# One core, a fused layer kernel: constants from two engines, other warm-up matmuls, an earlier load and a new list of steps

## The chip, the cores and the metric

The kernel runs on one core of a Trainium2 chip. The metric is the device time in microseconds, and the median of several runs is given. All data are float32. "us" is a microsecond.

## What is computed

Four sequences of 512 tokens with 256 features go through one layer. The tokens are taken in four chunks of 128, and each chunk depends on the one before it, since a small network of three weights per head is trained while the sequence is read. Cut to what matters:

```
xn   = layernorm(x)
qkv  = xn @ Wqkv                       # 4 heads of 64; also 2 heads of 128 for the window attention
q,k,v= silu(qkv); q,k = l2norm(q), l2norm(k)
lr   = softplus(xn @ Wlr + BASE_LR_INV); mom = sigmoid(xn @ Wm + bm)
for chunk in 4 chunks of 128 tokens:
    out  = (silu(q@W0.T) * (q@W2.T)) @ W1.T      # before the update
    dw0,dw1,dw2 = gradients(k, v, lr) + mean(mom) * M
    M = dw ; W = renorm(W + newton_schulz5(dw))  # five rounds of matmuls, 16 heads x 3 weights
ttt  = rms(out) * o_norm_g * silu(xn @ Ws + bs)
att  = windowed softmax attention (128 queries, 256 keys)
x    = x + layernorm((ttt + att) @ Wo)
x    = x + layernorm(gelu(layernorm(x) @ proj1.T + b1) @ proj2.T + b2)
```

## The kernel before, in words

Every engine runs the same hand-made list `ORDER` of about 690 steps in turn, and executes of each step only its own part: TensorE the matmuls, VectorE and ScalarE the evictions and elementwise work, GpSimd the powers (square roots are done there as `pow`) and some products. A step is named KIND.chunk.index. An engine that reaches a step whose inputs are not there waits, and all later steps of that engine wait behind it. `bank_plan` walks the same list and gives every matmul step one or two of the eight PSUM banks, those that are free the longest.

The steps of chunk 0 and the lines that matter here:

- LN1 (L1051 to L1062, GpSimd L1388 and L1393) takes the layer norm's statistics, LNX (L1068, L1075) normalizes, XT (L531, L538) transposes with `ident`, QK (L554) and VV (L563) are the projections. The VectorE part of VV (L1108, L1114) adds `small_bias` and so waits for seven small loads, counted in `ld_misc`.
- WI (L1334, L1338, ScalarE L1010) spreads the three weights, which six loads bring (`w_in`, shown as X), into W. SI (L861, L862) is the silu, NQ the sum of squares (ScalarE L874, VectorE L1120, GpSimd `pow` L1388), NR the reciprocal and the product (L1126, L1128, GpSimd L1388, shown as silu<-silu,rq). TR (L582) transposes, and VectorE copies six of the ten results (L1141).
- SP (L1046, written to `lr`) makes the learning rates. KL on GpSimd multiplies with them (shown as kl and vl). FW, DH, GB and OUT (L620, L608, L595, L634) are the forward pass and the gradients, EL and ELB (L1155, L1157, L1046, L1166) their elementwise part, DW (L653) the weight gradients, OE (L1180, L1191) and OY (L1199) the output, MU and MR (L1206, L1219) copy the gradients and take row sums, SS and SN (L1215, L1388 `fro`, L1224 to L1229) normalize them.
- TX, NA, NB, NX (L671, L680, L690, L702) are one Newton-Schulz round, five rounds for each of three weights. The VectorE part of NA is the write of A, which is the first reader of `eye`.
- F1 (L771) and F2 (L782) are the MLP, S and PT and PV (L721, L728, L737) the attention, WO, L2, NT (L752, L1319, L759) what lies between.

ScalarE has one function table loaded at a time. `table(name)` loads another where a step needs it: SILU for SI, GB, FW, EXP for SP and S, GELU for F1.

At the start GpSimd fills all constants (L1496 to L1514): the learning-rate bias, `ident`, `ones_blk`, `ones_avg`, `half`, `neg_half`, `mask`. The last fill raises `consts`, on which TensorE, ScalarE and VectorE wait before their first step. `wait_apart` also waits on `consts`. GpSimd then builds `eye` in four small sums before its first step. TensorE transposes `ident` 24 times (L797) before its first step. The sync queue issues, in this order, the rows and `wqkv`, small weights, seven small loads, the six weight loads (L468), `p1T`, `p2T`, `wo`, the rows again for the residual, and then the second chunk's rows (`rows_in(1)`, L483), once all of the first rows have been normalized.

Of the kernel before, what the change touches and what calls it, by code (L numbers as in the profile page):

```python
# [128 lines left out]
def steps(text):  # L129
# [12 lines left out]
    MR.0.0 MR.0.1 MR.0.2 OY.0 PT.0.1 QK.1.2 QK.1.3 SS.0.0 SS.0.1 PV.0.0 PV.0.1 S.0.2 S.0.3 VV.1.0 CT.0.0 CT.0.1 VV.1.1
    SS.0.2 SN.0.0 SN.0.1 SN.0.2 VV.1.2 PT.0.2 VV.1.3 WO.0.0 PT.0.3 TX.0.0.0 TX.0.0.1 TX.0.0.2 SI.1.0 SI.1.1 NA.0.0.0
    NA.0.0.1 NA.0.0.2 PV.0.2 PV.0.3 WON.0.0 WO.0.1 CT.0.2 NB.0.0.0 NB.0.0.1 NB.0.0.2 CT.0.3 WON.0.1 WO.0.2 WO.0.3
    NX.0.0.0 NX.0.0.1 NX.0.0.2 TX.0.1.0 TX.0.1.1 TX.0.1.2 WON.0.2 WON.0.3 L2.0.0 L2.0.1 L2.0.2 TR.1.0 TR.1.1 NA.0.1.0
    SI.1.2 NA.0.1.1 NA.0.1.2 NB.0.1.0 NB.0.1.1 NB.0.1.2 TR.1.2 TR.1.3 L2N.0.0 L2.0.3 L2N.0.1 L2N.0.2 NX.0.1.0 NX.0.1.1
    NX.0.1.2 NT.0.0 NT.0.1 NT.0.2 TX.0.2.0 TX.0.2.1 L2N.0.3 SM.1 TX.0.2.2 NT.0.3 LN1.2 NQ.1.0 SI.1.3 NA.0.2.0 NA.0.2.1
    NA.0.2.2 NQ.1.1 F1.0.0 F1.0.1 NB.0.2.0 NB.0.2.1 NB.0.2.2 LNX.2 NQ.1.2 NQ.1.3 F1.0.2 F1.0.3 NX.0.2.0 NX.0.2.1
    NR.1.0 NR.1.1 NX.0.2.2 NR.1.2 TX.0.3.0 F1.0.4 TX.0.3.1 TX.0.3.2 S.1.0 NA.0.3.0 NR.1.3 NA.0.3.1 KL.1.0 NA.0.3.2
    KL.1.1 F1.0.5 NB.0.3.0 NB.0.3.1 NB.0.3.2 NX.0.3.0 NX.0.3.1 NX.0.3.2 KL.1.2 TX.0.4.0 TX.0.4.1 TX.0.4.2 TR.1.4  # L150
    F1.0.6 MS.1 TR.1.5 TR.1.6 S.1.1 XT.2 TR.1.7 F1.0.7 NA.0.4.0 NA.0.4.1 NA.0.4.2 MM.1 NB.0.4.0 NB.0.4.1 SP.1 NB.0.4.2
# [82 lines left out]
def layer_kernel(nc, x, Wqkv, Wlr, Wm, bm, Ws, bs, Wo, w0, w1, w2, o_norm_g, qk_scale, qk_offset,  # L234
                 proj1T, proj1_bias, proj2T, proj2_bias, out):
    with ExitStack() as ctx:
# [15 lines left out]
        def sem(name):  # L252
            return ctx.enter_context(nc.semaphore(name))
# [1289 lines left out]
```

## Time and profile before

| | us |
|---|---|
| median of 3 runs | 389.87 |
| lowest, highest | 389.61, 390.98 |
| the profiled execution's own time | 389.76 |
| its span, first to last instruction | 388.0 |
| TensorE busy in it | 370.2 (95%) |
| VectorE busy | 268.7 (69%) |
| ScalarE busy | 223.0 (57%) |
| GpSimd busy | 189.7 (49%) |

A page of the profile lists the engines' busy time, the span in 40 slices, and the costliest groups of instructions. PE is TensorE's matmuls, PEld its weight loads, DVE is VectorE, ACT ScalarE, POOL GpSimd, SP the sync queue. A float32 matmul stands in the trace as two pieces, a transpose as one. A busy TensorE is not one at its peak, since the ends of matmuls are modelled: an overlapped piece counts as busy until its modelled end.

### The profile page before, as it was taken

To read this page: it belongs to the slowest core of one execution; us is meant where nothing else is said; L and a number is where in the kernel's file an instruction comes from. 1 tells how busy PE (TensorE), PEld (TensorE's weight loads), DVE (VectorE), ACT (ScalarE), POOL (GpSimd) and SP (SyncE) were. 2 spreads that over 40 slices of the span, in tenths; PEclk is the share of its full clock that TensorE was granted. 3 is DMA by queue.
4 is the path that set the end of the run, shared out by engine and by line. 5 is a ranking of instruction groups with operands and counts; after the bars stand their busy time and mean duration, and the time that the engine had idled before them with its cause. 6 is when DMAs were issued, how large, how long until landed. Compare 5 with 4: busy or idle time off the path is not lost.

```text
span 388.0 us, 15998 instructions
## 1 busy us (share of the span) xinstructions
PE 370.2 (95%) x6766; PEld 296.1 (76%) x6766; DVE 268.7 (69%) x720; ACT 223.0 (57%) x439; POOL 189.7 (49%) x274
## 2 busy tenths in 40 slices
PE   5877999999999999999999999999999999999994
PEld 5457768976878877889567898779887757988883
DVE  3479799875557679987737876986786783777024
ACT  2587666595873366658574356674369845624500
POOL 6189563646207663667635563452245440457114
PEclk9999999999999999999999999999999999999999
DMA  5862000000000000000040000000000020000101
GB/s 154 233 198 57 2 2 4 3 4 3 3 3 4 0 3 2 3 18 4 30 125 4 3 2 2 3 2 4 3 5 30 27 61 3 0 3 0 56 0 55
DMA packets 12342, 10.85 MB, mean 28 GB/s; under 512 B 4208, under 2 KB 11760, under 8 KB 12272
## 3 DMA queue, kind: packets, MB, share of 16 engines
q1 hardware_dynamic: 12272, 9.83, 8.4%
q8 instruction: 54, 0.88, 0.9%
q14 instruction: 16, 0.13, 0.1%
HBM read 7.73 MB, written 2.10 MB: 25 GB/s over the span
## 4 chain that ended last, share of the span: by engine, by line
PE 76%; DVE 11%; issue 4%; POOL 4%; SPq 3%; ACT 2%; DMA 1%; POOLq 0%; DVEq 0%; ACTq 0%
PE pair L771 14%; PE pair L782 13%; PE pair L702 6%; PE pair L690 6%; PE pair L680 6%; PE pair L671 5%; PE pair L752 4%; PE pair L582 3%; PE pair L563 2%; PE pair L737 2%; PE pair L721 2%; PE pair L554 2%; POOL fro L1388 2%; PE pair L620 1%; DVE h L1046 1%
## 5 line engine op out<-in xcount | busy, mean ns | idle before, releaser
L771 PE MATMUL pair<-xn2T,p1T 128*128 128x512 f32 (+1 forms) x160 | 59.0, 513 | 0.0
L782 PE MATMUL pair<-p2T,h 128*128 128x256 f32 x256 | 56.7, 379 | 0.0
L782 PEld LDWEIGHTS pair<-p2T,h 128*128 128x128 f32 x256 | 48.2, 190 | 6.4
L1393 POOL TENSOR_SCALAR var<-mv 128x1 f32<-128x1 f32 (+1 forms) x55 | 13.0, 236 | 70.0 <-DVE mv L1357 31.5
L1022 ACT ACTIVATE h<-pair,b 128x512 f32<-128x512 f32 (+1 forms) x40 | 24.0, 602 | 31.8 <-PE pair L771 31.7
L771 PEld LDWEIGHTS pair<-xn2T,p1T 128*128 128x128 f32 x160 | 28.9, 190 | 17.0 <-issue 14.8
L813 ACT ACT_TABLE_LOAD x29 | 37.2, 1283 | 2.2 <-PEq L1533 1.7
L1046 DVE SCALAR_TENSOR_TENSOR A<-pair,eye 128x512 f32<-128x512 f32 x45 | 28.3, 682 | 10.3 <-PE pair L680 10.0
L1388 POOL TENSOR_TENSOR rstd<-var,neg_half 128x1 f32<-128x1 f32 (+1 forms) x55 | 32.8, 596 | 4.6
L1046 DVE SCALAR_TENSOR_TENSOR B<-pair,eye 128x512 f32<-128x512 f32 x45 | 28.4, 683 | 7.2 <-PE pair L690 7.2
L1388 POOL TENSOR_TENSOR nq<-ssq,half 128x8 f32<-128x8 f32 (+1 forms) x16 | 23.6, 1485 | 15.6 <-DVE ssq L1120 15.6
L554 PE MATMUL pair<-wqkv,xnT 128*128 128x512 f32 x64 | 29.8, 600 | 0.4 <-ACT xnT L806 0.4
L690 PEld LDWEIGHTS pair<-A 64*64 64x64 f32 x1440 | 23.6, 134 | 6.9 <-issue 4.2
L947 ACT ACTIVATE X<-pair 128x512 f32<-128x512 f32 x36 | 19.7, 601 | 15.1 <-PE pair L702 15.0
L702 PEld LDWEIGHTS pair<-X,B 64*64 64x64 f32 x1440 | 23.4, 134 | 6.1 <-issue 4.6
L690 PE MATMUL pair<-A 64*64 64x64 f32 x1440 | 25.9, 221 | 0.7 <-issue 0.4
L806 ACT ACTIVATE XT<-pair 128x512 f32<-128x512 f32 x45 | 24.2, 609 | 4.2 <-PE pair L671 4.1
L680 PEld LDWEIGHTS pair<-XT 64*64 64x64 f32 x1440 | 22.6, 135 | 4.8 <-issue 4.4
L702 PE MATMUL pair<-X,B 64*64 64x64 f32 x1440 | 25.6, 221 | 0.2
L1388 POOL TENSOR_TENSOR kl<-silu,lr 128x256 f32<-128x256 f32 x24 | 14.4, 621 | 23.0 <-issue 23.0
L680 PE MATMUL pair<-XT 64*64 64x64 f32 x1440 | 24.7, 220 | 0.3 <-DVE rows_b L1046 0.2
L671 PE MATMUL pair<-ident,X 128*128 128x128 f32 x180 | 23.4, 276 | 0.0
(164 smaller groups left out, 783.1 us busy)
## 6 DMA issues: line engine op xcount, KB each, us to landing
x<-in_L_attn_x_dram SPq DMA_DIRECT2D x4, 512.0 KB, 4.7
out_dram<-rows_a SPq DMA_DIRECT2D x16, 128.0 KB, 1.7
x_in<-in_L_attn_x_dram SPq DMA_DIRECT2D x3, 512.0 KB, 4.9
p1T<-in_L_ffn_proj_dram SPq DMA_DIRECT2D x1, 1024.0 KB, 5.4
p2T<-in_L_ffn_proj_dram SPq DMA_DIRECT2D x1, 1024.0 KB, 7.8
wqkv<-in_L_attn_Wqkv_dram SPq DMA_DIRECT2D x1, 768.0 KB, 4.6
x_in<-in_L_attn_x_dram SPq DMA_DIRECT2D x4, 128.0 KB, 4.3
wo<-in_L_attn_Wo_dram SPq DMA_DIRECT2D x1, 256.0 KB, 8.0
```

The source lines that it names most:

```text
L554: mm_ = pe.matmul(ps, xnT[:, k, b * P:(b + 1) * P], wqkv[:, k, 0:512], start=(k == 0), stop=(k == KC - 1))
L671: mm_ = pe.transpose(ps[:, b * P:(b + 1) * P], X[:, g, 2 * b:2 * b + 2, :], ident[:, :])
L680: mm_ = pe.matmul(BANK[bank[0] + row][64 * col:64 * col + 64, n * HD:(n + 1) * HD], xt, xt, start=True, stop=True)
L690: mm_ = pe.matmul(BANK[bank[0] + row][64 * col:64 * col + 64, n * HD:(n + 1) * HD], a, a, start=True, stop=True)
L702: mm_ = pe.matmul(BANK[bank[0] + row][64 * col:64 * col + 64, n * HD:(n + 1) * HD], B[64 * row:64 * row + 64, g, 4 * (row ^ (slot & 1)) + ...
L771: mm_ = pe.matmul(ps[:, at], p1T[:, k, n * P:(n + 1) * P], xn2T[:, k, at], start=(k == 0), stop=(k == KC - 1))
L782: mm_ = pe.matmul(ps[:, 0:DIM], h[:, n, b * P:(b + 1) * P], p2T[:, n, :], start=(n == 0), stop=(n == HC - 1))
L806: return act.activation(dst, src, ACT.Copy)
L813: act.preload_act_table_set(name)
L1022: act.activation(h[:, n, at], BANK[bank[0]][:, at], ACT.Gelu, bias=b1[:, n:n + 1]).then_inc(S["h"].sem, 1)
L1046: return dve.scalar_tensor_tensor(out=out_, in0=in0, scalar=scalar, in1=in1, op0=op0, op1=op1)
L1388: return pool.tensor_tensor(out_, in0, in1, op)
```

## The change

Constants. `ones`, a new 128x128 tile, is filled by VectorE, which then raises `warm`. VectorE also fills `neg_half`, `half`, `small_bias`, `ones_avg` and the four quarters of `ones_blk`, and raises `prepared`. GpSimd fills `ident` alone, selects its diagonal and raises `consts`. It then makes `mask` and raises `masks`, and waits for `prepared` before its first step. ScalarE and VectorE no longer wait for `consts` at the start. The build of `eye` becomes a step of its own, EY.0, between OE.0 and SS.0.0 on GpSimd. Where the other constants are read first, a wait is added: SS.0.0 on TensorE (`prepared`), VV.0.0 on VectorE (`prepared`), S.0.0 on VectorE (`masks`).

Warm-up. TensorE waits for `warm` and does 8 matmuls of `ones` with itself, in place of 24 transposes of `ident`, and then waits for `consts`.

Loads. `rows_in(1)` is issued behind the six weight loads and ahead of `p1T`.

List. All 686 steps of before remain, in another order, with EY.0 added. Of the start: WI.0 goes from before LN1.0.3 to behind NQ.0.1 on VectorE, and from before SI.0.0 to behind QK.0.3 on ScalarE; LN1.0.3 comes before LNX.0.1; LN1.1 comes before NQ.0.2 on GpSimd; SP.0 goes from before S.0.0 to behind TR.0.9 on VectorE; OUT.0 comes before QK.1.0 to QK.1.2; OE.0 comes before ELB.0.0; OY.0 comes before MR.0.0; PV.0.2, PV.0.3 and MS.1 come before the first A, WO.0.0 behind it. With the rules of `table` the list of before needs 29 table loads and the new one 26.

```diff
@@ sync @@
             sp.wait_ge(ld_qkv, 16)
...
+            rows_in(1)
             sp.dma_start(p1T[:, :, :], proj1T.rearrange("(k p) n -> p k n", p=P)).then_inc(ld_p1, 16)
...
-            rows_in(1)
             sp.wait_ge(*S["x_again"](0, 16))
@@ tensor @@
+                if c == 0 and g == 0:
+                    pe.wait_ge(prepared, 1)
...
+            pe.wait_ge(warm, 1)
+            for n in range(8):
+                pe.matmul(BANK[7][:, (n % 4) * P:(n % 4 + 1) * P], ones[:, :], ones[:, :], start=True, stop=True)
             pe.wait_ge(consts, 1)
-            for n in range(24):
-                pe.transpose(BANK[7][:, (n % 4) * P:(n % 4 + 1) * P], ident[:, :], ident[:, :])
             run(ORDER)
@@ scalar @@
-            act.wait_ge(consts, 1)
             run(ORDER)
@@ vector @@
+                    if c == 0:
+                        dve.wait_ge(prepared, 1)
                     dve.wait_ge(ld_misc, MISC)
...
+                if c == 0 and b == 0:
+                    dve.wait_ge(masks, 1)
...
-            dve.wait_ge(consts, 1)
+            dve.memset(ones[:, :], 1.0).then_inc(warm, 1)
+            dve.memset(neg_half[:, :], -0.5)
+            dve.memset(half[:, :], 0.5)
+            dve.memset(small_bias[:, 0:12], BASE_LR_INV)
+            dve.memset(ones_avg[:, :], 0.5 / CHUNK)
+            for r in range(2):
+                for k in range(2):
+                    last = dve.memset(ones_blk[64 * r:64 * r + 64, 64 * k:64 * k + 64], float(r == k))
+            last.then_inc(prepared, 1)
             run(ORDER)
@@ gpsimd @@
+            def EY(c):
+
+                pool.wait_ge(consts, 1)
+                for b in range(BATCH):
+                    last = tt(eye[:, b, :], ident[:, 0:HD], ident[:, HD:P], ALU.add)
+                last.then_inc(eyes, 1)
...
+            pool.memset(ident[:, :], 0.0).then_inc(zeroed, 1)
             pool.wait_ge(zeroed, 1)
             pool.affine_select(out=ident[:, :], in_=ident[:, :], compare_op=ALU.not_equal, fill=1.0, base=0,
-                               pattern=[[-1, P]], channel_multiplier=1)
-
+                               pattern=[[-1, P]], channel_multiplier=1).then_inc(consts, 1)
+            pool.memset(mask[:, :], 0.0).then_inc(zeroed, 1)
+            pool.wait_ge(zeroed, 2)
...
+                               pattern=[[1, P]], channel_multiplier=-1).then_inc(masks, 1)
+            pool.wait_ge(prepared, 1)
             run(ORDER)
```

The start of the list, before and after:

```diff
-    LN1.0.0 LNX.0.0 LN1.0.1 XT.0.0 XT.0.1 LN1.0.2 LNX.0.1 QK.0.0 LNX.0.2 XT.0.2 WI.0 LN1.0.3 VV.0.0 LNX.0.3 SI.0.0
-    QK.0.1 VV.0.1 NQ.0.0 SI.0.1 VV.0.2 NQ.0.1 XT.0.3 QK.0.2 VV.0.3 NR.0.0 NR.0.1 SI.0.2 NQ.0.2 MS.0 SM.0 LN1.1 QK.0.3
+    XT.0.0 LN1.0.0 LNX.0.0 LN1.0.1 LN1.0.2 QK.0.0 LN1.0.3 LNX.0.1 XT.0.1 SI.0.0 LNX.0.2 LNX.0.3 VV.0.0 QK.0.1 XT.0.2
+    VV.0.1 NQ.0.0 XT.0.3 SI.0.1 VV.0.2 NQ.0.1 QK.0.2 SI.0.2 QK.0.3 WI.0 NR.0.0 NR.0.1 TR.0.0 LN1.1 VV.0.3 NQ.0.2
...
```

## Rows read from the trace of the kernel before

**Rows 1.** The page: busy us of each engine, share of the span, instructions.

```profile
PE 370.2 (95%) x6766; PEld 296.1 (76%) x6766; DVE 268.7 (69%) x720; ACT 223.0 (57%) x439; POOL 189.7 (49%) x274
```

**Rows 2.** Windows: start and end, length, busy us of each engine, granted clock, DMA.

```profile
0.00:60.00 60.00, 49.44 (x518) 37.12 (x519) 42.48 (x125) 36.73 (x81) 38.41 (x60) 1.00 0.36 104
60.00:290.00 230.00, 229.22 (x5079) 185.31 (x5078) 173.21 (x449) 139.87 (x267) 112.89 (x152) 1.00 0.03 10
290.00:303.00 13.00, 12.45 (x415) 9.96 (x414) 9.02 (x24) 11.84 (x25) 5.97 (x8) 1.00 0.10 34
```

**Rows 3.** Chain that ended last, first 60 us: start, length, what.

```profile
11.44 2.22 DMA X<-in_L_attn_w_dram
...
18.77 3.27 POOL nq L1388 x2
...
49.87 1.78 DVE M L1206 x3
```

**Rows 4.** Timeline 0 to 20: start, length, engine, line, idle before and its releaser.

```profile
1.66 1.28 ACT L813 ACT_TABLE_LOAD   x1 [1.66 <-PEq L1533]
...
3.73 0.43 DVE L1051 BATCH_NORM_STATS2 st<-x_in 128x6 f32<-128x256 f32 x1 [3.73 <-POOL ones_blk L1514]
...
7.58 0.47 SPq L463 DMA_DIRECT2D b<-in_L_ffn_proj_bias_dram  x1
...
8.39 0.60 PE L531 MATMUL pair<-ident,rows_b 128*128 128x128 f32 x4
...
13.69 0.63 DVE L1334 COPY W<-X 128x128 f32<-128x128 f32 x4 [4.43 <-DMA X<-in_L_attn_w_dram]
...
16.04 0.63 ACT L861 ACTIVATE silu<-raw 128x512 f32<-128x512 f32 x1
```

**Rows 5.** Windows over the warm-up's matmuls (L797) alone.

```profile
4.00:7.60 3.60, 3.60 (x18) 1.00 0.79 233
7.80:8.50 0.70, 0.70 (x7) 1.00 0.17 58
```

**Rows 6.** DMA issues with us to landing, the one issued at 7.58.

```profile
b<-in_L_ffn_proj_bias_dram SPq DMA_DIRECT2D x1, 4.0 KB, 3.6
```

**Rows 7.** Line L1388, 18 to 33 us: ns min/median/max, first and last start.

```profile
L1388 POOL TENSOR_TENSOR nq<-ssq,half x4: 1633/1646/1652, 18.8 to 28.0; 128x8 f32<-128x8 f32 x4
L1388 POOL TENSOR_TENSOR silu<-silu,rq x4: 1040/1042/1044, 22.0 to 31.0; 128x512 f32<-128x512 f32 x4
L1388 POOL TENSOR_TENSOR rstd<-var,neg_half x1: 1063/1063/1063, 26.9 to 26.9; 128x4 f32<-128x4 f32 x1
```

**Rows 8.** Timeline 20 to 60.

```profile
22.07 1.00 DVE L1126 TENSOR_SCALAR nqe<-nq 128x8 f32<-128x8 f32 x1 [0.16 <-POOL nq L1388]
...
33.51 3.68 DVE L1141 COPY tttT<-pair 128x512 f32<-128x512 f32 x6
...
34.28 1.19 POOL L1388 TENSOR_TENSOR kl<-silu,lr 128x256 f32<-128x256 f32 x2
...
41.01 0.69 DVE L1155 TENSOR_TENSOR h<-A,pair 128x512 f32<-128x512 f32 x1 [2.32 <-ACT h L904]
...
54.77 1.13 DVE L1046 SCALAR_TENSOR_TENSOR rows_b<-pair,rsums,y 128x128 f32<-128x128 f32 x4
54.78 3.23 POOL L1388 TENSOR_TENSOR fro<-ss,half 128x8 f32<-128x8 f32 x2 [2.66 <-DVE ss L1215]
```

**Rows 9.** Timeline 55 to 76.

```profile
62.15 1.65 PE L680 MATMUL pair<-XT 64*64 64x64 f32 x96
...
62.99 1.89 DVE L1046 SCALAR_TENSOR_TENSOR A<-pair,eye 128x512 f32<-128x512 f32 x3
```

**Rows 10.** Timeline 284 to 304.

```profile
295.32 0.42 DVE L1275 CUSTOM_DVE_ANT_0 masked<-pair,mask 128x256 f32<-128x256 f32 x1 [0.69 <-issue]
...
295.64 1.28 ACT L813 ACT_TABLE_LOAD   x1
```

**Rows 11.** Timeline 340 to 360.

```profile
354.02 0.41 PE L759 MATMUL pair<-ident,rows_b 128*128 128x128 f32 x2 [0.33 <-DVE rows_b L1326]
```

More of the change, by code:

```diff
@@ L142 @@
[L142 to L151, printed above, removed]
@@ new lines @@
+    WON.0.1 CT.0.3 SI.1.3 WO.0.2 NX.0.0.0 NX.0.0.1 WO.0.3 NX.0.0.2 SM.1 WON.0.2 WON.0.3 TX.0.1.0 TR.1.0 TX.0.1.1
+    TX.0.1.2 L2.0.0 L2.0.1 MM.1 NA.0.1.0 NA.0.1.1 NA.0.1.2 NB.0.1.0 NB.0.1.1 L2N.0.0 TR.1.1 TR.1.2 NB.0.1.2 TR.1.3
+    NX.0.1.0 NX.0.1.1 L2.0.2 L2.0.3 NX.0.1.2 NT.0.0 NT.0.1 NT.0.2 TX.0.2.0 TX.0.2.1 L2N.0.1 L2N.0.2 L2N.0.3 TX.0.2.2
+    NT.0.3 NA.0.2.0 NA.0.2.1 NA.0.2.2 F1.0.0 F1.0.1 NB.0.2.0 NB.0.2.1 NB.0.2.2 F1.0.2 NQ.1.0 NQ.1.1 F1.0.3 LN1.2
+    NX.0.2.0 NX.0.2.1 NX.0.2.2 TX.0.3.0 TX.0.3.1 F1.0.4 TX.0.3.2 NQ.1.2 F1.0.5 NA.0.3.0 NR.1.0 NA.0.3.1 NA.0.3.2
@@ new lines @@
+    L2N.1.2 TX.1.2.0 TX.1.2.1 TX.1.2.2 L2N.1.3 NT.1.1 NT.1.2 NT.1.3 NQ.2.1 NA.1.2.0 NA.1.2.1 NA.1.2.2 SI.2.2 SI.2.3
+    F1.1.0 F1.1.1 NQ.2.2 NQ.2.3 NB.1.2.0 NB.1.2.1 NB.1.2.2 MS.2 F2N.0.0 F2N.0.1 F1.1.2 F1.1.3 F2N.0.2 NX.1.2.0 F2N.0.3
+    NR.2.0 SM.2 NX.1.2.1 NX.1.2.2 TX.1.3.0 TX.1.3.1 TX.1.3.2 F1.1.4 NA.1.3.0 NA.1.3.1 NR.2.1 NR.2.2 NR.2.3 NA.1.3.2
+    F1.1.5 NB.1.3.0 NB.1.3.1 NB.1.3.2 MM.2 NX.1.3.0 NX.1.3.1 NX.1.3.2 LN1.3 TX.1.4.0 TX.1.4.1 TX.1.4.2 TR.2.4 TR.2.5
+    KL.2.0 KL.2.1 SP.2 NA.1.4.0 NA.1.4.1 NA.1.4.2 TR.2.6 F1.1.6 LNX.3 NB.1.4.0 NB.1.4.1 NB.1.4.2 TR.2.7 F1.1.7 MP.2
@@ L184 @@
+    WO.3.2 CT.3.3 WON.3.0 WON.3.1 L2.3.0 L2.3.1 L2N.3.0 L2N.3.1 F2.2.2 F2.2.3 NT.3.0 NT.3.1 WO.3.3 WON.3.2 WON.3.3
+    L2.3.2 L2.3.3 L2N.3.2 L2N.3.3 F1.3.0.0 F2N.2.0 F2N.2.1 F2N.2.2 F2N.2.3 F1.3.1.0 F1.3.2.0 F1.3.3.0 F1.3.4.0
+    F1.3.5.0 NT.3.2 F1.3.6.0 NT.3.3 F1.3.7.0 F1.3.0.1 F1.3.1.1 F1.3.2.1 F1.3.3.1 F1.3.4.1 F2.3.0 F1.3.5.1 F1.3.6.1
+    F1.3.7.1 F2N.3.0 F2.3.1 F2.3.2 F2N.3.1 F2N.3.2 F2.3.3 F2N.3.3
 """)
@@ L401, in layer_kernel @@
         consts = sem("consts")
+        prepared = sem("prepared")
+        masks = sem("masks")
+        warm = sem("warm")
         eyes = sem("eyes")
@@ L1509, in _ @@
             pool.affine_select(out=mask[:, 2 * P:3 * P], in_=mask[:, 2 * P:3 * P], compare_op=ALU.is_ge, fill=NEG, base=0,
-                               pattern=[[1, P]], channel_multiplier=-1)
-            pool.memset(ones_blk[0:64, 0:64], 1.0).then_inc(zeroed, 1)
-            pool.wait_ge(zeroed, 2)
-            pool.memset(ones_blk[64:128, 64:128], 1.0).then_inc(consts, 1)
-            pool.wait_ge(consts, 1)
-            for b in range(BATCH):
-                last = tt(eye[:, b, :], ident[:, 0:HD], ident[:, HD:P], ALU.add)
-            last.then_inc(eyes, 1)
+                               pattern=[[1, P]], channel_multiplier=-1).then_inc(masks, 1)
+            pool.wait_ge(prepared, 1)
             run(ORDER)
```

80 lines of the change are left out of this document (36 added, 44 removed).

## The prediction

> **What bounds the kernel now.** I read the page first: TensorE is busy 370.2 us, 95% of the span of 388.0, and idle 17.8 [rows 1]. The windows say where. In the first 60 us TensorE lacks 10.6, from 60 to 290 it lacks 0.8 of 230, in 290 to 303 it lacks 0.5 [rows 2], and so about 5.9 are left for the end. Busy is overstated where pieces wait for each other, but the places are clear: time can be won at the start, a little at 290 to 303, and at the end. Elsewhere only a list that makes TensorE wait more, or less, can move anything.
>
> The chain of waits tells who rules the start. It runs over the sync queue's issues to the six weight loads, the last issued at 11.44 and landing 2.22 later, from there through WI and the silu to GpSimd's `pow` at 18.77, and at 49.87 it is still on VectorE (copies of M) [rows 3]. The timeline shows why: VectorE stood still 4.43 us in front of WI.0, with LN1.0.3 and the VV copies behind it, and the first silu came at 16.04 [rows 4].
>
> **The change part by part.** The sum is against the profiled execution's 389.76, which is 0.11 below the median of 389.87. I add 0.11 at the end.
>
> *Constants.* VectorE's first step began at 3.73, released by GpSimd's last fill [rows 4]. Now nine fills of its own stand in front of it. The trace shows no fill on VectorE. Its queue has more to do first than ScalarE's, which was free at 1.66 [rows 4], so I put it at 2.1 to 2.7, and I bound the fills by nothing and by half the 0.43 of its first statistics each: 2.1 to 4.6, likely 3.7, so no gain and at worst 0.9 lost there. Both ends stay hidden, as the next paragraphs show. The three added waits are for things ready by then, with tens of microseconds of cover at S.0.0 and SS.0.0. At VV.0.0 all later steps of VectorE, and ScalarE's first silu, are queued behind the wait, but the wait on the small loads next to it ends later.
>
> *Warm-up.* 24 pieces held TensorE until the first real transpose at 8.39 [rows 4]. They went 18 in 3.6 us, 0.20 each, and then 7 in 0.7, 0.10 each, while the clock column says 1.00 for both [rows 5]. By the pace that is the 1.2 GHz level up to about 7.7 us and the 2.4 GHz level after about 4 us of work. The new warm-up is 8 float32 matmuls, 16 pieces, at 0.20 about 3.3 us, from about 2.9 to 6.2. The first transpose comes 2 us earlier. Some early matmuls may run at half pace.
>
> *Where that gain stops.* The first silu needs VV.0.0's copy, and that needs the seventh small load, issued at 7.58 and landed 3.6 later [rows 4, 6]: 11.2. The projections are ready before that: QK.0.0 from 7.3, four pieces of 512 columns at 0.10 per 128 columns [rows 5], 1.7, then XT.0.1, then VV.0.0 with four of 276 columns, 0.9, so 10.4 with the gaps. So the silu starts at about 11.4 and not at 16.04, 4.6 earlier. It is WI.0's move that gives this, not the warm-up. On ScalarE two copies now come before the squares, so the first `pow` starts at 14.9, not 18.77: 3.9 earlier.
>
> *GpSimd to the last product.* Four `pow` at 1.65, four products at 1.04, and LN1.1's root, 1.06 and with the sum ahead of it about 1.3, are 12.1 [rows 7]. WI.0 (0.63 [rows 4] and two larger copies, about 1.4) now lies before NR.0.0 on VectorE, and LN1.1 stands before the third `pow`, which has to wait for it: together about 2.5 of gaps where before there were 1.2. The last product ends at 29.5, before at 32.0. Gain left: 2.5. The second chunk's rows, issued at about 12.1 behind the weights, are there in time, and `p1T` has 60 us of cover.
>
> *To the gradients.* The six copies that started at 33.51 start at 31.2, and the first EL at 38.7 and not 41.01 [rows 8]: 2.3 left. SP.0 is now behind these copies. KL, which waits for it, starts at 35.1, not 34.28 [rows 8], 0.8 later. KL is four times 1.19 and about 0.6, 7.1, and GpSimd's part of EL about 2.5: 44.7. That is still ahead of VectorE, whose copies of M began at 49.87 [rows 3] and now begin at about 48.
>
> *VectorE to the first A.* From 41.01 to 62.99 [rows 8, 9] VectorE is full (42.5 busy of 60, with most of the idle time before 16 [rows 2]). A gain in latency is here worth what VectorE has less to do. The new list puts PV.0.2 and PV.0.3 (two sequences, 1.13 [rows 8]) and MS.1 (about 0.4) ahead of the first A and takes WO.0.0 (0.6) away, 0.9 more. With MR waiting for OY the first A comes at 62.5. TensorE starts the round at 61.1 and not 62.15 [rows 9] and, since 0.9 of VectorE's work is already done, stays ahead. I book 1.3, with ends 0 and 2.4. EY.0, four sums, sits on GpSimd between OE.0 and SS.0.0, where GpSimd was idle 2.66 us before `fro` [rows 8]; it costs nothing, or its own 1.2 if that cover goes.
>
> *Chunk 2.* In before, S.3.0 stood in the fourth round: VectorE waited 0.69 for its scores with A queued behind, and ScalarE loaded a table at 295.64 inside the same round, while it was busy 11.84 of 13 [rows 2, 10]. The new list has S.3.0 in the fifth round, behind the last copies that the round needs from ScalarE. I book 0.6, with ends -1.5 (the loads now hold F1's banks) and 1.5.
>
> By the Trainium skill's page "ScalarE: Activation LUTs", section "What ACT_TABLE_LOAD costs", a switch takes a drain beside the load, about 2.66 us in all. The trace shows 1.28 [rows 10]. Three loads fewer are 3.8 us of ScalarE by the row and 8.0 by the page; at the page's price the sum would be about 1 us lower.
>
> *Chunk 3.* TensorE waited 0.33 for L2N.3.2 at 354.02 [rows 11]. The new list sends NT.3.2 behind six F1 halves. I book 0.1, with ends 0 and 0.4. The last steps behind F2.3.3 are unchanged.
>
> *The rest of the list* moves a few hundred steps by one to ten places over 230 us in which TensorE is full. I book 0, with ends -1.5 and 1.5.
>
> Sum: 389.76 - 1.3 - 0.6 - 0.1 = 387.76, plus 0.11 gives 387.9.
>
> **The rivals.**
>
> *A, the start's gain is absorbed.* VectorE is full from the first EL to the first A, and the order there costs what the latency saves. For it: my first A is only 0.5 earlier. Against it: TensorE needs less from VectorE after that. Booked 0.3 in place of all: 389.6, from 388.9 to 390.9.
>
> *B, the gain survives in full.* The 2.4 us at EL reach the first round, since VectorE's work between can be packed closer, and chunk 2 gives 1.5: 389.87 - 2.4 - 1.5 = 386.0, from 385 to 387.
>
> *C, slower: the clock.* The new warm-up ends at 6.2, and TensorE then has small gaps while rows come in. Between 6.4 and 18.3 it has 11 us of matmuls at full pace, nearly no slack. Each microsecond that it stays at the pace of the first row [rows 5] costs half a microsecond. The first 1 us of delay has cover; from about 12 on the start's gain of 1.3 is used up. At full pace only from 18.3 (12 us at half pace, 6 lost, 1 covered, with 1.3 and 0.7 won) the time is 389.9 + 5 - 2.0 = 392.9. For it: 24 pieces in a row came before the rise, now 16 with a gap after. Against it: the work goes on with gaps under 1 us.
>
> *D, shared reads.* A small VectorE instruction took 1.00 us at 22.07 for eight columns, about as long as the GpSimd product of 1.04 that ran beside it [rows 7, 8]. EY.0 and the later KL now run beside VectorE's fullest stretch. If these eight products and sums hold it 1.2 us, the start keeps 0.1: 389.1. The Trainium skill's page "GPSIMD Engine Reference", in its table of the engine, names the SBUF interfaces as shared with VectorE for instructions with two SBUF inputs; the row agrees that something is shared.
>
> **How the numbers follow.** Forecast, 0.38: 387.9, its own range 387.2 to 388.9. A 0.22 at 389.6. B 0.25 at 386.0. C 0.11 at 392.9. D 0.04 at 389.1. Half a per cent, about what a measurement tells from no change, is 1.95 us: faster means below 387.9. Half of the forecast's case and B are faster, 0.44. The other half, A and D are the same, 0.45. C is slower, 0.11. The range leaves out C and the lowest third of B, under 0.2: 385.3 to 390.9.
>
> **What would show it.** The first silu at 11 to 12 us; the last product at 29 to 30; the six copies of 33.51 at 31; the first A within 0.7 us of 62.99, lower; WI.0 without the 4.43 idle; 26 table loads; a round in chunk 2 without the 0.69; TensorE's pieces at 0.10 per transpose before 10 us. A first A later than 63, or QK.0.2 taking 3.6 us and not 1.9, would make the forecast wrong on the slow side. A first A at 61 would make it B.

## The result, and the profile after

The changed kernel took 387.73 us in the median of five executions (387.30 to 388.49), beside 389.87 for the kernel before (389.43 to 390.98). The ratio is 0.9943, with a 95% interval of 0.9929 to 0.9958. The profiled execution is the 388.49 one, with a span of 386.7. It is the slowest of the five. Twelve more executions of the same kernel, taken later and told below as e5, gave a median of 389.1 (387.01 to 391.41) beside 389.44, a ratio of 0.9984 (0.9962 to 1.0006), which does not exclude that nothing was won. There the new kernel's executions lie 4.4 us apart and the old one's 2.4 (389.00 to 391.36, 23 executions); this document explains only a part of that.

The page of the new kernel: busy us of each engine, and the table loads.

```profile
PE 369.2 (95%) x6758; PEld 294.9 (76%) x6758; DVE 271.5 (70%) x729; ACT 219.2 (57%) x436; POOL 191.7 (50%) x267
...
L820 ACT ACT_TABLE_LOAD x26 | 33.4, 1283 | 2.1 <-PEq L1548 1.7
```

Windows of the new kernel, with the columns of [rows 2].

```profile
0.00:60.00 60.00, 51.04 (x555) 38.62 (x559) 45.61 (x147) 40.04 (x87) 38.38 (x53) 1.00 0.35 104
60.00:290.00 230.00, 227.01 (x5073) 182.55 (x5064) 174.35 (x438) 130.76 (x255) 117.70 (x157) 1.00 0.05 15
290.00:303.00 13.00, 13.00 (x398) 10.91 (x397) 7.33 (x20) 11.50 (x24) 4.72 (x6) 1.00 0.02 4
```

Beside [rows 2], TensorE is 1.6 us busier in the first 60 us and busy through all of 290 to 303, but from 60 to 290 it now lacks 3.0 of 230, where before it lacked 0.8. The timeline of the first 61 us shows the new start: start, length, engine, line, what, and in brackets the idle time before and who ended it.

```profile
2.76 0.17 DVE L1389 MEMSET ones<- 128x128 f32 x1 [2.76 <-issue]
3.06 3.75 PE L803 MATMUL pair<-ones 128*128 128x128 f32 x16 [3.06 <-DVE ones L1389]
6.61 0.55 PE L535 MATMUL pair<-ident,rows_b 128*128 128x128 f32 x2
7.73 1.96 PE L558 MATMUL pair<-wqkv,xnT 128*128 128x512 f32 x4 [0.57 <-ACT xnT L813]
11.57 0.63 ACT L868 ACTIVATE silu<-raw 128x512 f32<-128x512 f32 x1 [0.98 <-DVE small L1122]
15.06 3.44 POOL L1406 TENSOR_TENSOR nq<-ssq,half 128x8 f32<-128x8 f32 x2 [5.41 <-DVE ssq L1128]
16.66 0.63 DVE L1344 COPY W<-X 128x128 f32<-128x128 f32 x4
...
27.78 1.04 POOL L1406 TENSOR_TENSOR silu<-silu,rq 128x512 f32<-128x512 f32 x1 [0.34 <-DVE rq L1136]
30.19 3.68 DVE L1149 COPY tttT<-pair 128x512 f32<-128x512 f32 x6
34.12 1.20 POOL L1406 TENSOR_TENSOR kl<-silu,lr 128x256 f32<-128x256 f32 x2 [3.07 <-issue]
37.68 0.69 DVE L1163 TENSOR_TENSOR h<-A,pair 128x512 f32<-128x512 f32 x1 [2.50 <-ACT h L911]
46.47 1.89 DVE L1214 COPY M<-pair 128x512 f32<-128x512 f32 x3
47.42 1.15 POOL L1406 TENSOR_TENSOR eye<-ident 128x64 f32<-128x64 f32 x4
...
59.63 1.67 PE L686 MATMUL pair<-XT 64*64 64x64 f32 x96
60.77 1.88 DVE L1052 SCALAR_TENSOR_TENSOR A<-pair,eye 128x512 f32<-128x512 f32 x3
```

WI.0's copies (16.66) no longer have 4.43 us of idle time in front of them, the first silu comes at 11.57 and not at 16.04 [rows 4], and TensorE's first round starts at 59.63, not at 62.15 [rows 9].

A ledger is the main tool from here on. It takes the start of the first NA piece of chunks 0, 1 and 2, the last F2 piece of chunk 2 and the last of chunk 3, from each kernel's timeline, and gives the first of these times and the four stretches between them. Chunk 3's column ends with its last F2 piece; about 6 us follow in every kernel. A profile is one execution; the median of all executions stands beside it, and beside that the median of before, measured together with it.

```
                 to NA.0.0  chunk 0  chunk 1  chunk 2  chunk 3   sum    median  before
before              62.15   100.32   100.06    90.34    29.15  382.02   389.87
after               59.63   101.60   101.72    88.34    29.46  380.75   387.73  389.87
e1  new code only   62.25   101.28    99.93    91.70    29.14  384.30   392.32  389.57
e2                  62.16   100.84    99.82    91.71    29.15  383.68   391.08  389.57
e3                  61.55   101.16   104.69    90.35    29.15  386.90   391.03  389.57
e4                  59.45   101.61   102.25    90.35    29.15  382.81   391.16  389.57
e5  after again     59.70   101.11   101.01    88.64    29.46  379.92   389.10  389.44
e6  S.3.0 back      63.08   101.07   100.90    92.99    29.46  387.50   394.89  389.44
e7  new from c2     62.64   100.32   100.29    88.50    29.46  381.21   388.92  389.44
e8  old start       63.13   102.22   101.09    88.75    29.45  384.64   392.30  389.44
e9  new list only   63.89   101.65   103.05    88.64    29.45  386.68   392.96  389.67
e10 MM.2 behind     59.70   101.13   101.05    88.13    29.46  379.47   388.39  389.67
e11 start and c2    60.48   101.31   100.04    88.16    29.46  379.45   387.08  389.67
e12 16 warm-ups     62.02   100.30    99.55    90.94    29.14  381.95   391.14  390.13
```

After against before: 2.5 won up to the first round, 1.3 lost in chunk 0, 1.7 lost in chunk 1, 2.0 won in chunk 2, 0.3 lost in chunk 3. Together 1.3 are won. The same kernel's other execution, e5, lost 0.8 and 0.95 in chunks 0 and 1 and won 2.1 in all, so one trace is good to about 1 us there.

The stretches do not hold the same work, since a new order moves steps across their ends. TensorE in chunk 2's stretch, of before and of after (start and end, length, busy us and pieces, clock, DMA): first everything, then the WO pieces (L752, L758), then the PV pieces (L737, L743).

```profile
262.53:352.87 90.34, 89.79 (x1892) 1.00 0.05 15
262.95:351.29 88.34, 88.34 (x1892) 1.00 0.05 15
...
262.53:352.87 90.34, 7.77 (x32) 1.00 0.05 15
262.95:351.29 88.34, 5.68 (x24) 1.00 0.05 15
...
262.53:352.87 90.34, 5.29 (x40) 1.00 0.05 15
262.95:351.29 88.34, 6.17 (x48) 1.00 0.05 15
```

Two WO steps have left the stretch and one PV step has come in, 1.2 us of work less. So of the 2.0 some 0.8 are a gain of chunk 2 itself; TensorE's idle time there went from 0.55 to nothing. One of the two WO steps lies now in chunk 3's stretch (four pieces, 1.03 busy), which is why that one is 0.3 longer although its idle time, 0.33 before, is gone too.

### The profile page after: what moved, and what is told of

Read it like the earlier page. It is cut to its first block, busy times and chain, and to the rows that moved or that the text cites. A ratio compares the mean times of both kernels' runs of the same rounds, so it can differ in the third digit from the quotient of the medians.

```text
span 386.7 us, 15982 instructions
## 1 busy us (share of the span) xinstructions
PE 369.2 (95%) x6758; PEld 294.9 (76%) x6758; DVE 271.5 (70%) x729; ACT 219.2 (57%) x436; POOL 191.7 (50%) x267
## 4 chain that ended last, share of the span: by engine, by line
PE 83%; DVE 8%; issue 3%; POOL 3%; ACT 2%; POOLq 0%; DVEq 0%; ACTq 0%
PE pair L788 14%; PE pair L777 14%; PE pair L708 6%; PE pair L686 6%; PE pair L696 5%; PE pair L677 5%; PE pair L558 5%; PE pair L743 3%; PE pair L586 3%; PE pair L758 3%; PE pair L567 3%; PE pair L727 3%; PE pair L734 2%; PE pair L657 2%; PE pair L624 1%
## 5 line engine op out<-in xcount | busy, mean ns | idle before, releaser
L1411 POOL TENSOR_SCALAR var<-mv 128x1 f32<-128x1 f32 (+1 forms) x55 | 14.1, 256 | 67.4 <-DVE mv L1367 30.5
L1406 POOL TENSOR_TENSOR fro<-ss,half 128x8 f32<-128x8 f32 x9 | 15.9, 1781 | 13.4 <-DVE ss L1223 13.4
```

The lines of the kernel that those rows point to most:

```text
L1406: return pool.tensor_tensor(out_, in0, in1, op)
```

## Experiments

The first four take the change apart. In all kernels with the new code and an old piece of list, EY.0 stands ahead of SS.0.0.

**e1: the new code, the old list.**

```diff
 # after's code
-ORDER = steps("""... the new list ...""")
+ORDER = steps("""... the old list, EY.0 ahead of SS.0.0 ...""")
```

> All of the change but the list: constants from two engines, 8 matmuls on ones, the earlier load of the second chunk's rows, with the list of before (EY.0 put ahead of SS.0.0). Theory, the move of WI.0 makes the start faster: here WI.0 still waits for the weights ahead of the first silu, so the silu stays at 16.0 us and the time at 389.8, within 0.4 of before. Rival, the shorter warm-up and the free GpSimd make the start faster: the first silu comes before 15 us and the time is 388.8 or less.

Measured: 392.32 (391.32 to 394.79), ratio 1.0074 (1.0046 to 1.0102). The start is as before. The loss sits in a few holes within groups of TensorE's pieces. Timeline of e1, TensorE alone:

```profile
73.67 1.50 PE L686 MATMUL pair<-XT 64*64 64x64 f32 x84
75.73 0.39 PE L686 MATMUL pair<-XT 64*64 64x64 f32 x10 [0.57 <-issue]
...
296.35 1.61 PE L686 MATMUL pair<-XT 64*64 64x64 f32 x92
299.33 0.33 PE L686 MATMUL pair<-XT 64*64 64x64 f32 x4 [1.36 <-issue]
```

84 pieces of one group of 96, then nothing for 0.57 us, then the rest: no wait of the program lies between them. "issue" says that nothing in the profile released the engine. With the old list the new code makes no part of the gain, and its loss is of a kind that the prediction did not have.

**e2: the same, with WI.0 behind NQ.0.1.**

```diff
 # e1's list
-... WI.0 LN1.0.3 VV.0.0 ... NQ.0.1 XT.0.3 ...
+... LN1.0.3 VV.0.0 ... NQ.0.1 WI.0 XT.0.3 ...
```

> As e1_code_only, with WI.0 alone moved behind NQ.0.1 in the list. Theory, WI.0's move is what wins the start: the first silu is at 11.4 to 12.5 us, GpSimd's last product before 30, the first round of Newton-Schulz starts 1.5 to 2.5 us before 62.15, and the time is 387.8 to 388.4. Rival, VectorE is full from the first EL on, and the gain is lost there unless the order of OE, OY and PV changes too: first round within 0.8 of 62.15, time 389.2 or more.

Measured: 391.08 (390.33 to 393.77), ratio 1.0039 (1.0021 to 1.0057). The first silu came at 12.39, but the first round at 62.16. The first silu is what the theory had, the first round (within 0.8 of 62.15) and the median (389.2 or more) are what the rival had. In this execution TensorE ran from 20 to 24 us at a granted clock of 0.59, so the trace may understate what moving WI.0 alone gives. The median is 1.2 below e1's, and the intervals of the two ratios overlap.

**e3: the new list up to NA.0.0.0, the old one behind. e4: the new list up to TX.2.0.0.**

```diff
 # e3: after's code
-ORDER = the new list
+ORDER = the new list up to NA.0.0.0, then the other steps in the old order
 # e4: after's code
-ORDER = the new list
+ORDER = the new list up to TX.2.0.0, then the other steps in the old order
```

> The changed kernel, with its new list up to the first NA.0.0.0 and all steps behind it in the order of before. Theory, the start's 2.5 us at the first round are kept where the rest of the list stays: first round at 59.6, time 387.4. Rival, TensorE's stream absorbs a part whatever the rest: time 388.5 or more.

> The changed kernel with its new list up to the first TX.2.0.0 and the order of before behind it, so chunk 2's rounds and chunk 3 are as before. Theory, the new order in chunk 2's rounds won 2 us (its profile is 0.4 behind at the third chunk's first round and 1.6 ahead at its end): time 389.5, 1.8 above the changed kernel. Rival, the 0.4 behind comes from one stall of 2 us at 203 us that this execution happened to have, and chunk 2 is worth 0.6 as booked: time 388.3.

Measured: e3 391.03 (389.29 to 394.65), ratio 1.0037 (1.0012 to 1.0061); e4 391.16 (390.20 to 394.51), ratio 1.0057 (1.0032 to 1.0082). The profiled execution of e3 was its slowest, with the clock at 0.50 from 28 to 32 us and a hole of 2.17 us at 180, so its medians count. The new start is worth 1.3 against e1, and there too the intervals overlap. In e3 WO.0.0 stands ahead of the first NA step, where after has it behind: of the 1.9 by which the first round is later than in after, 0.9 are this step. In e4 everything is as in after up to chunk 2, which then takes 90.35 and not 88.34, as in before. From e4 to after the sum falls by 2.1: that is what the new order behind TX.2.0.0 is worth, over chunks 2 and 3 and the end of chunk 1 together. e3's median falls to its rival (388.5 or more), and e4's lies above both its cases (389.5 and 388.3).

**e5: after once more, unchanged. e6: S.3.0 back in the fourth round.**

```diff
 # e6: after's list
-... TX.2.3.2 TR.3.3 SI.3.1 ... TX.2.4.2 NR.3.0 NR.3.1 NR.3.2 S.3.0 NR.3.3 ...
+... TX.2.3.2 TR.3.3 S.3.0 SI.3.1 ... TX.2.4.2 NR.3.0 NR.3.1 NR.3.2 NR.3.3 ...
```

> The kernel after once more, unchanged, beside the three below on one chip. In its first trace TensorE stood 2.0 us in front of NX.1.3.0 at 205.72, released by nothing that the profile shows (issue). Theory 1: this stall belongs to the program (its code and its place in the instruction stream); then it is there again within 0.3 us of its length and the median is again 387.3 to 388.2. Rival: it is an accident of one execution; then it is gone, the profiled span is 384.5 to 385.5, and the median, which is over many executions, stays at 387.3 to 388.2.

> The kernel after with one step moved: S.3.0 goes from the fifth round of chunk 2 (behind NR.3.2) back into the fourth (behind NA.2.3.0 and TR.3.3), near where the kernel before has it; nothing else differs. Theory S (the 2.0 us that chunk 2 wins are S.3.0's): the milestones are those of after up to the start of NA.2.3, from there to NA.2.4 it takes 0.7 to 2.0 us longer, a table load lies inside the fourth round again, 27 loads or more in all, and the median is 388.8 to 389.8. Rival R (the gain comes from the many small moves in chunk 2, not from this step): less than 0.5 us is lost, median 387.5 to 388.3.

Measured: e5 389.10 (387.01 to 391.41), which is 0.9 above both its cases; the hole is there again at the same piece, but with 1.32 us and not 2.03. e6 394.89 (393.00 to 396.07), ratio 1.0127 (1.0100 to 1.0153). One step in another place costs 5.8 us in the medians, three times what I had expected at most. Timeline of e6 around the fourth round, all engines:

```profile
298.53 1.28 ACT L820 ACT_TABLE_LOAD   x1
298.66 1.10 PE L727 MATMUL pair<-akT,aqT 128*128 128x256 f32 x4 [1.06 <-ACT akT L897]
...
302.02 1.28 ACT L820 ACT_TABLE_LOAD   x1
...
303.31 0.42 ACT L866 ACTIVATE silu<-raw 128x256 f32<-128x256 f32 x1
...
304.21 0.42 DVE L1128 TENSOR_REDUCE ssq<-y 128x4 f32<-128x256 f32 x1 [2.15 <-ACT y L881]
...
305.42 1.28 ACT L820 ACT_TABLE_LOAD   x1
305.79 1.88 DVE L1052 SCALAR_TENSOR_TENSOR B<-pair,eye 128x512 f32<-128x512 f32 x3
306.62 1.60 PE L708 MATMUL pair<-X,B 64*64 64x64 f32 x76 [1.80 <-DVE B L1052]
```

Three table loads lie in one round, where after has one, at 298.06, and the next at its very end, at 303.66. Before had two inside the round, at 295.64 and 298.66: the silu of chunk 3, which brings the middle load here, lay ahead of S.3.0 there. VectorE stands 2.15 us in front of `ssq`, since ScalarE's square behind the load at 302.02 is late. The three B steps are queued behind `ssq`, and TensorE waits 1.80 for B. The loads did not become more, there are still 26: where they stand makes the price. Chunk 2 takes 4.4 to 4.7 us longer than in the two traces of after. The rest of this trace's loss lies at the start, where the program is the same as in e5, instruction for instruction:

```profile
7.81 3.75 PE L558 MATMUL pair<-wqkv,xnT 128*128 128x512 f32 x4 [0.56 <-ACT xnT L813]
```

```profile
28.00:32.00 4.00, 3.13 (x20) 2.86 (x19) 3.49 (x16) 3.89 (x9) 3.65 (x4) 0.62 0.48 131
32.00:36.00 4.00, 4.00 (x21) 3.85 (x19) 3.44 (x6) 2.79 (x9) 1.00 (x1) 0.53 0.01 4
```

QK.0.0 takes 3.75 where it took 1.96 in after: half pace, so the 1.2 GHz level, though the clock column has 1.00 there for both. Later the column has 0.62 and 0.53 (windows of TensorE's busy time and the other columns as in [rows 2]). The first round starts 3.4 us later than in e5.

**e7: the old list up to TX.2.0.0, the new one behind. e8: the old list up to NA.0.0.0, the new one behind.**

```diff
 # e7: after's code
-ORDER = the new list
+ORDER = the old list up to TX.2.0.0, then the other steps in the new order
 # e8: after's code
-ORDER = the new list
+ORDER = the old list up to NA.0.0.0, then the other steps in the new order
```

> After's code, the old list up to TX.2.0.0 (EY.0 ahead of SS.0.0), the new list behind: the mirror of e4_new_to_c2. If chunk 2's order is worth 2.0 us on its own, independent of what lies before it, this is e1_code_only's 392.3 less 2.0: 390.3 (389.6 to 391.0), and from NA.2.0 to the last F2.2.3 it takes 88.0 to 88.7 us, as in after (88.34), not 90.3. If the 2.0 us come only from how the new list hands chunk 2 over (steps done ahead in chunk 1), it takes over 89.5 and the median is above 391.2.

> After's code, the old list up to NA.0.0.0 (with EY.0 ahead of SS.0.0), the new list behind: the mirror of e3_new_start. It takes the new order of the start away alone. The first NA piece comes at about 62.2 and not 59.6. Theory 1 (half of the start's 2.5 us survives, as e3 against e1 had it: 1.3): median 388.6 to 389.5. Rival A (the later rounds absorb it, the start's order is worth nearly nothing): 387.6 to 388.4. Rival B (it survives in full): 389.9 to 390.7.

Measured: e7 388.92 (388.02 to 390.12), ratio 0.9982 (0.9967 to 0.9997); e8 392.30 (391.29 to 394.03), ratio 1.0072 (1.0047 to 1.0096). Chunk 2 takes 88.50 in e7, as the expectation had it, whatever lies before it, and e7 has no hole over 0.6 us, so not e1's at 75.73 either, though it has e1's program up to there. Its median lies 0.7 under the expectation's range, which was built on e1's 392.3 and so on its holes. e8 is 3.2 above e5 on the same chip, more than any of its three cases: its first round is 3.4 later, and chunk 0 takes 1.1 more, with a wait of 1.3 for A at 66 in it. Of the 3.4, 0.9 come on top of e1's, and these are PV.0.2 and PV.0.3, which e8 has ahead of the first NA step and e1 behind it (eight pieces, 0.99). QK.0.0 took 3.25 us, again at half pace for a while, but the first silu came at 16.12 in both: the wait for the weights covered it. So the start's new order is worth 1.3 by e3 and up to 3.2 by e8.

**e9: the new list with the code of before. e10: MM.2 behind NX.1.3.0. e11: new start and new chunk 2, old middle.**

```diff
 # e9: before's code
-ORDER = the old list
+ORDER = the new list without EY.0
 # e10: after's list
-... NB.1.3.2 MM.2 NX.1.3.0 NX.1.3.1 ...
+... NB.1.3.2 NX.1.3.0 MM.2 NX.1.3.1 ...
 # e11: after's code
-ORDER = the new list
+ORDER = the new list up to NA.0.0.0, the old one up to TX.2.0.0, the new one behind
```

> The mirror of e1_code_only: the code of before (24 transposes on the identity, GpSimd fills the constants, second chunk's rows behind the MLP weights), with the new list, without EY.0, which that code does not have. e1_code_only was 2.7 us above before on its chip although its start was as before. Theory K (the new code by itself costs about 2 us, in front of any list): this is 2 us under after's 387.7 to 389.1, 385.7 to 387.1. Rival N (the code costs nothing; e1's 2.7 us were TensorE's instruction stalls, which depend on program and list together and don't add up): 387.5 to 389.2, as after, at most 0.7 above for a start that the long warm-up makes later (first transpose at 8.4, not 6.6).

> The kernel after with one step moved by one place: MM.2 behind NX.1.3.0, as in before, and not ahead of it; this also gives NX.1.3.0 a bank pair that was long free. All five traces with the new list in this place have TensorE standing 1.3 to 2.0 us between MM.2's pieces and NX.1.3.0, and none with the old list there has it. Theory M (the place of MM.2 makes the stall): NX.1.3.0 starts 0.1 to 0.4 us behind the last NB piece, from NA.1.3 to NA.1.4 it takes 9.6 to 10.0 us, not 10.6 to 11.3, and the median is 0.7 to 1.3 us below after's, 386.7 to 388.2. Rival I (it is a stall of the instruction supply, whatever step stands there): it stays at that point of the program, over 1 us, and the time is after's, 387.7 to 389.1.

> After's code, the new list for the start (to NA.0.0.0), the old one for the rounds of chunks 0 and 1 (to TX.2.0.0), the new one behind: the two parts that gained, without the part that gave back 3 us. Theory P (parts add up): the first NA piece at 59.5 to 59.9, from there to the last F2 piece 318.6 us as in e7_new_from_c2, 378.3 in all against 380.75 in after and 382.0 in before; median 385.3 to 387.0, below both kernels. Rival A (TensorE's first round starts early but VectorE has the same work to do before chunk 1, so the old middle absorbs it): from NA.0.0 on it takes 320 or more, median 387.5 to 389.5.

Measured: e9 392.96 (392.07 to 394.43, and one execution of 398.74 at a mean clock of 0.94), ratio 1.0062 (1.0041 to 1.0084). Both theories fell, and the timeline says why:

```profile
13.80 0.63 ACT L861 ACTIVATE silu<-raw 128x512 f32<-128x512 f32 x1 [0.82 <-DVE small L1114]
...
24.11 1.41 DVE L1058 BATCH_NORM_STATS2 st<-x_in 128x6 f32<-128x256 f32 x4 [1.93 <-DMA x_in<-in_L_attn_x_dram]
...
30.08 1.33 PE L538 MATMUL pair<-ident,rows_b 128*128 128x128 f32 x5 [4.31 <-DVE rows_b L1075]
```

The new list asks for the second chunk's rows at LN1.1, and in the old code they come behind the MLP weights. VectorE waits for them with VV.0.3's copies queued behind, TensorE waits 4.31, and the first round starts at 63.89. The warm-up's 24 pieces cost it the start as well (the first silu at 13.80, not 11.57). Code and list are one change: each alone is slower than before.

e10: 388.39 (387.22 to 390.87, and one execution of 945.83), ratio 0.9974 (0.9952 to 0.9995). The hole did not go with MM.2:

```profile
203.06 0.33 PE L708 MATMUL pair<-X,B 64*64 64x64 f32 x5
204.27 0.68 PE L708 MATMUL pair<-X,B 64*64 64x64 f32 x27 [0.88 <-issue]
```

It stands at the same place of TensorE's stream, one piece further, now in the middle of a group, where no wait of the program lies. Theory M fell and rival I held, with 0.88 in place of over 1.

e11: 387.08 (385.69 to 389.85), ratio 0.9936 (0.9913 to 0.9960). That is below both kernels' medians, 0.1 above theory P's range and under rival A's. By its ratio it is below e5's 0.9984, but not clearly below the 0.9943 of after's first five executions. The first round came at 60.48 and not at 59.5 to 59.9, since WO.0.0 stands ahead of it here as in e3, and the rest took 318.97, near the expectation's 318.6. The gains of the start and of the order behind TX.2.0.0 add up.

**e12: before, with TensorE's stream as short as in e1.**

```diff
             pe.wait_ge(consts, 1)
-            for n in range(24):
+            pe.wait_ge(consts, 1)
+            for n in range(16):
 ...
+                if c == 0 and g == 0:
+                    pe.wait_ge(consts, 1)
                 pe.wait_ge(*S["mom_ss"](c, g + 1))
```

> The kernel before, its list and all its engines as they were, except that TensorE's instruction stream is given the length that it has in e1_code_only: 16 warm-up pieces and not 24, and the two extra waits (on a signal long set). In e1_code_only, 2.3 to 2.7 us slower than before with the same list, the start was as before and the time went in stalls inside groups of TensorE's pieces (0.76 us at 74.9, 0.52 at 78.9, 1.56 at 297.8), where nothing that the profile shows was waited for. Theory L (where the instructions lie in TensorE's stream decides these stalls; another count in front of all of them moves them): this kernel has them too, at the same pieces as e1, and the median is 391 to 392.5. Rival T (it is the traffic or the timing that the other code changes bring, the second chunk's rows ahead of the weights above all): no such stalls at those pieces, median 389.0 to 390.0, as before. The first transpose comes at about 7.6 to 8.0 in place of 8.39 and changes nothing behind 16 us, where the weights of the memory are waited for.

Measured: 391.14 (389.73 to 395.04), ratio 1.0035 (1.0013 to 1.0057). Its profiled execution was the fastest of twelve and has none of e1's holes; the others go up to 392.3, and one to 395.0. So eight pieces fewer at the head and two waits more cost about 1.0 us by the medians, but no trace shows where. Theory L has the median and not the holes, rival T the reverse. This stays open.

## Why the prediction was right, and where it was not

The 387.9 was met (387.73), and e5's 389.1 also lies in the range. That it was met to 0.2 is luck, twice over. In the two profiled executions 1.3 are won and not the 2.0 of the sum, and two errors met in that: the start brought 1.2 more than booked and chunks 2 and 3 together 1.0 more, and the middle took 2.9 that was booked at nothing. And the medians of the first five executions are 2.1 apart, those of e5 0.3.

*What bounds the kernel.* Half right. Time was won at the start and around 290 to 303, as named; the end gave nothing. "In 60 to 290 it lacks 0.8" says that nothing can be won there, and hid that this stretch can lose.

*Constants.* Forecast 3.7 for the first statistics, with 2.1 to 4.6; they began at 3.51, behind `ones` at 2.76. Right, and without effect that shows.

*Warm-up.* 3.06 to 6.6, first transpose at 6.61, 1.8 earlier: nearly as written.

*Where that gain stops.* The time was right (11.4, measured 11.57), its reason half wrong. I had written that WI.0's move gives this and not the warm-up. e9 has the new list with the old warm-up, and there the first silu comes at 13.80, since QK.0.0 has to wait for 24 warm-up pieces. Counted in this order, of 4.5 us the list gave 2.2 and the new code, by its shorter warm-up, the other 2.2; counted the other way, e1's silu comes at 16.12 and the code alone gives nothing. For the whole each needs the other. The step that failed is "not the warm-up": that the projections are ready before the small loads was worked out for the new warm-up only.

*To the first A.* First `pow` 14.9 (15.06), last product ends 29.5 (28.82), copies 31.2 (30.19), EL 38.7 (37.68), KL 35.1 (34.12), M about 48 (46.47), first A 62.5 (60.77), first round 61.1 (59.63). The order of the links held, and each from the EL on came 1.0 to 1.7 earlier than written. The gaps on GpSimd were 1.7 of the 2.5 that I gave them, and the EL gained 3.3 and not 2.3. From the EL to the first A it took 23.09, where before had 21.98 [rows 8, 9]: 1.1 were lost there, about the 0.9 of the moved steps, but not the 1.8 that 62.5 amounts to. So rival B's time at the first round came, and its "packed closer" did not; the wait of MR for OY seems priced too high, and the latency ahead of the EL won more. The start brought 2.5 where 1.3 was booked, just over its bound of 2.4. Rival A fell by the traces, though e5's median of 389.1 lies in its range.

*EY.0 and rival D.* The three copies of M took 1.89 with EY.0's sums beside them [the rows of 46.47 and 47.42] and 1.78 without [rows 3]: 0.1, not 1.2. D fell. Of what the Trainium skill's page "GPSIMD Engine Reference", section "1. Specifications", calls shared this stretch shows only that much.

*Chunk 2.* The stretch took 2.0 less, with 0.6 booked and 1.5 the bound, but 1.2 of that is work that moved out of it. What is left, 0.8, and the idle time, 0.55 to nothing, fit the 0.6. That it was S.3.0's move is not shown: after differs from e4 in the whole order behind TX.2.0.0, and no run moved S.3.0 alone among its old neighbours. e6 shows what the step costs among the new ones, 4.4 to 4.7 in the traces: a table load in the middle of the round delays ScalarE's square, that delays `ssq`, and B is queued behind. Before had no silu behind S.3.0 in that round and not this chain.

*Table loads.* The Trainium skill's page "ScalarE: Activation LUTs", section "What ACT_TABLE_LOAD costs", would add a drain to each load. In e6 ScalarE loads at 302.02 for 1.28, and its next step starts at 303.31: nothing beside the load, and the rows decide. Nor does the count carry the gain: e11, the fastest, has 30, and e4, slower than before, has 25.

*Chunk 3.* 0.1 gain forecast; the stretch is 0.3 longer in every trace with the new order there. Its idle time went from 0.33 to nothing, as forecast, and a WO step moved in.

*The rest of the list.* This is the step that failed: booked at 0, ends 1.5 either way, measured 2.9 lost in after and 1.7 in e5. Most of it are two holes. Timeline of after in chunk 1:

```profile
201.80 1.68 PE L696 MATMUL pair<-A 64*64 64x64 f32 x96
202.56 1.89 DVE L1052 SCALAR_TENSOR_TENSOR B<-pair,eye 128x512 f32<-128x512 f32 x3
203.41 0.29 PE L549 MATMUL pair<-ms,ones_avg 128*64 128x8 f32 x4
...
205.72 1.63 PE L708 MATMUL pair<-X,B 64*64 64x64 f32 x96 [2.03 <-issue]
```

The first B was ready at 203.2, and TensorE stood until 205.72; the other hole is 0.57 at 73.23. Before had one, of 0.42. The section below says what comes with these holes. e11, with the old middle, lies 1.3 below e10, which has the new one, by the medians, with overlapping intervals.

*Rival C, the clock.* Its mechanism is real. It did not decide the median: in both traces of after QK.0.0 took 1.96 and 1.98. But e6, with the same program there, had 3.75, and in e2, e3, e6, e7 and e9 the clock column falls again somewhere between 16 and 36 us, while [rows 2] and e5 have 1.00. At the first round that is 1.1 us in e3 (against e11, which has the same steps up to there) and 3.4 in e6, of the size of the distance between e5's 387.0 and 391.4. I had given the late rise one price; it is a share of the executions that pays it. Of e5's twelve executions three have a mean granted clock of 0.988 or 0.989, and they took 389.2, 390.4 and 391.4; the nine others, at 0.995 or more, took 387.0 to 390.1, with a median of 389.0. So falls of the clock do not make e5's median, and what makes it 1.3 above the first five's is open: the mean clock does not show a late rise, and only one of the twelve was profiled.

## What to carry to other kernels

A table load of ScalarE can cost several times its own length where VectorE's next step waits for ScalarE and a third engine's next input is queued behind that step (e6); follow what is queued behind it. A ledger by stretches compares like with like only if the pieces in each are counted, since a new order moves work across their ends. A list and the order of its loads belong together: take one alone and both may lose. And where TensorE issues hundreds of small pieces, book a loss or a spread of 1 to 3 us, as here, for a change of its instruction stream, since holes can appear in it that no wait explains.

## What the runs showed of the chip that was not expected

TensorE's holes come with its instruction loading. The page counts 54 packets of kind instruction on one queue, 0.88 MB, so 16 KB each. Laid beside TensorE's 6758 pieces, one comes every 125 pieces in the mean, each of which has its weight load. From the records of all traces, these are the holes of over 0.85 us, start to start, between the first round and the end; pieces are counted from 0, and before, e7 and e12 have none. Left out are three that a wait explains: in e6 at 297.3 (`akT`) and at 304.2 (B), in e8 at 65.5 (A).

```
          hole after piece   packet begins, ends     hole ends   later by
after          3807           203.25    204.25        205.72       1.5
e5             3807           202.25    203.25        204.59       1.3
e4             3807           202.80    203.84        205.29       1.5
e6             3807           205.34    206.32        207.81       1.5
e8             3807           206.89    207.94        209.21       1.3
e9             3809           207.09    208.09        209.41       1.3
e9             1067            78.52     79.40         80.99       1.6
e10            3808           201.87    202.86        204.27       1.4
e1             5797           296.96    297.91        299.33       1.4
e2             5797           296.27    297.34        298.70       1.4
e3             3058           176.96    178.29        179.96       1.7
e11             941            71.48     72.36         73.72       1.4
```

In all seven traces with the new list in chunk 1 the piece is the same to two, whatever step stands on it, and every hole ends 1.3 to 1.7 us after a packet. e9 has eight pieces more at its head, and its hole stands at the same count and so at an earlier step. Smaller holes stand at the same counts under the old list: 0.42 us idle after 3808 in before, 0.51 there in e3, and 0.57 after 941 in e1 as in e4 and after. So the place goes by the count in TensorE's stream, and neither by the step nor by the list; whether there is a hole differs from trace to trace. In e4, e5, e6 and e8 the profile puts the hole at 3807 down to VectorE's B, but NX.1.3.0 needs only the first of three, which in e5 was ready at 202.8; the third was at 204.0. The packet in front of it is late: in after 207 pieces have passed since the one before, in e5 171, in e10 141. At that time two loads of 512 KB issued at 198.0 and 198.5, the third chunk's rows for the residual and the fourth chunk's rows, fill the queues (after, 202.4 to 203.2, and the packet's own window, 203.2 to 204.3; queue and kind, packets, MB, share of 16 engines):

```profile
q1 hardware_dynamic: 214, 0.21, 73.4%
```

```profile
q1 hardware_dynamic: 37, 0.03, 8.6%
q8 instruction: 1, 0.02, 5.6%
```

The Trainium skill's page "Runtime: NRT & Kernel Launch", section "Instruction fetch mechanics", states that an engine's instructions are fetched in blocks of 16 KiB, 256 instructions, while the one before runs, at a cost that is mostly hidden. The trace agrees on the size. In stretches of small pieces, 17 ns each with their weights, it was not always hidden: up to 2.2 us at a block. That the holes are waits for these blocks is read from the table and not tested by a run of its own. That the row traffic delays the packet is likely for the seven holes near 3808 and not shown; the other five, in e1, e2, e3, e9 and e11, have none beside them, and no run moved the traffic alone.

TensorE's pace can differ between two executions of one program from 8 us on, as e5 and e6 show, which have the same instructions there: QK.0.0 took 1.98 and 3.75 us, and from 28 to 36 us the clock column has 1.00 in e5 and 0.62 and 0.53 in e6. In the 4 us before that fall TensorE was busy for 1.99 us in e5 and 1.75 in e6.
